# Causal attention: masking on GpSimd two units at a time, both maxima in one VectorE operation

## The reference

```
q, k, v = x @ Wq, x @ Wk, x @ Wv          # 8 batches, 16 heads of 16
dist = clip(abs(r[None, :] - r[:, None]), 0, 16)
scores = (q @ k.T) * rel_emb[dist]
scores = where(key > query, -inf, scores)
attn = softmax(scores / sqrt(16))
return (attn @ v) @ Wo + bo               # added to x, after a layernorm of x
```

## Time and profile before

| | us |
|---|---|
| median of 3 runs (3155.25 to 3163.49) | 3161.79 |
| the profiled execution's own time | 3150.57 |
| its span | 3148.8 |
| causal attention in it, first unit's scores to last | 2295.6 to 2816.7 |

### The profile page before, as it was taken

How to read it: one execution, slowest core, us unless ns; L and a number is a source line. 1 busy time by engine, 2 the same in 40 slices (tenths; PEclk the granted TensorE clock), 3 DMA queues, 4 the chain that set the end, 5 groups by cost and what they waited for, 6 DMA issues and landing times. The chain is left out here.

```text
span 3148.8 us, 54094 instructions
## 1 busy us (share of the span) xinstructions
PE 2839.0 (90%) x19481; PEld 2042.4 (65%) x19481; DVE 1666.4 (53%) x4549; ACT 1539.0 (49%) x2605; POOL 1306.5 (41%) x1303
## 2 busy tenths in 40 slices
PE   4899999758889988678999997999879999989999
PEld 3799999733344443358999996666546666655666
DVE  4411111178888888463111111666676666655666
ACT  1133333239999998311333332333257777772333
POOL 3544444349998889254444442000044444320000
PEclk9899999979999999868999998999989999998999
DMA  8199999711655555752999996000152344201000
GB/s 284 41 306 327 329 327 325 234 30 18 64 63 62 62 63 62 96 198 86 328 327 326 327 326 203 1 0 0 32 124 72 87 96 101 72 1 38 13 13 20
DMA packets 359857, 431.97 MB, mean 137 GB/s; under 512 B 86193, under 2 KB 314566, under 8 KB 356550
## 3 DMA queue, kind: packets, MB, share of 16 engines
q1 hardware_dynamic: 335046, 395.30, 45.5%
q0 software_dynamic: 24576, 33.57, 5.0%
HBM read 355.93 MB, written 72.88 MB: 136 GB/s over the span
## 5 line engine op out<-in xcount | busy, mean ns | idle before, releaser
L1675 ACT ACTIVATE f_h_t<-f_h_ps,f_b_t 128x128 f32<-128x128 f32 x1024 | 320.2, 364 | 596.3 <-PE f_h_ps L1633 596.3
L2062 POOL TENSOR_TENSOR a_dmg_buf<-a_c 128x2048 f32<-128x2048 f32 x128 | 520.1, 4091 | 85.2 <-DVE a_c L2544 42.7
L1633 PEld LDWEIGHTS f_h_ps<-f_rows_t,f_w 128*128 128x128 f32 x4096 | 481.4, 193 | 9.9 <-issue 3.5
L1633 PE MATMUL f_h_ps<-f_rows_t,f_w 128*128 128x128 f32 x4096 | 482.6, 276 | 2.3 <-DVE f_rows_t L1687 1.2
L1647 PE MATMUL f_y_ps<-f_w,f_h_t 128*128 128x256 f32 x2048 | 483.4, 379 | 0.0
L1593 POOL DMA_INDIRECT acc_rows<-f_y,f_give x128 | 205.1, 1603 | 487.2 <-DMA acc_rows<-f_y,f_give 451.6
L1647 PEld LDWEIGHTS f_y_ps<-f_w,f_h_t 128*128 128x128 f32 x2048 | 369.8, 190 | 39.9
L1687 DVE COPY f_rows_t<-f_t_ps 128x256 f32<-128x256 f32 x128 | 54.4, 425 | 598.4 <-PE f_t_ps L1621 593.7
L2411 DVE SCALAR_TENSOR_TENSOR a_bond_buf<-a_a,a_small_rep,a_q_ps 128x512 f32<-128x512 f32 x512 | 346.8, 740 | 5.3 <-PE a_q_ps L2238 2.2
L428 DVE SCALAR_TENSOR_TENSOR x_resid<-f_y_ps,f_gate,x_resid 128x256 f32 x512 | 218.8, 479 | 161.1 <-PE f_y_ps L311 155.5
L885 ACT ACTIVATE a_prob<-a_prob,a_neg_top 128x384 f32<-128x384 f32 (+3 forms) x512 | 276.5, 569 | 47.9 <-POOL a_neg_top L702 47.7
(11 more groups left out here) (337 smaller groups left out, 4110.4 us busy)
## 6 DMA issues: line engine op xcount, KB each, us to landing
f_w<-in_L_ffn_w_dram SPq DMA_DIRECT2D x256, 1024.0 KB
a_skewed<-skew SPq DMA_DIRECT2D x32, 512.0 KB, 7.2
a_k_s<-parts SPq DMA_DIRECT2D x16, 768.0 KB, 7.9
acc_rows<-x_resid SPq DMA_DIRECT2D x17, 512.0 KB, 5.3
xn_rows<-f_xn SPq DMA_DIRECT2D x16, 512.0 KB, 3.0
x_resid<-acc_rows SPq DMA_DIRECT2D x16, 512.0 KB, 8.3
a_vals<-val_rows SPq DMA_DIRECT2D x64, 128.0 KB, 4.2
skew<-a_bond SPq DMA_DIRECT2D x128, 64.0 KB
```

The lines of the kernel that those rows point to most:

```text
L1633: last = nc.tensor.matmul(h_ps[n // HB][:, (n % HB) * P:(n % HB + 1) * P], w1_sb[s][:, c, n * P:(n + 1) * P], rows_t[e % 2][:, c, :], star ...
L1675: nc.scalar.activation(h_t[k][:, n, :], h_ps[n // HB][:, (n % HB) * P:(n % HB + 1) * P], ACT.Gelu, bias=b1_t[:, n, e:e + 1]).then_inc(gelu ...
L2062: nc.gpsimd.tensor_tensor(dmg_buf[n % RING][:, :, :], places(c_sb[h], first_place(dg)), c_sb[h][:, PAD:].unsqueeze(1).broadcast_to([P, DG, ...
```

## The change

TensorE's mask product goes, and with it the masks in bfloat16. VectorE's `multiply` writes unmasked scores in two instructions: the keys left of the diagonal block with their maximum as before (not for t=0, which has none), and the diagonal block by a plain product. The maximum of the left part is put into the slot of `prob` itself, in the column just behind the block (a slot is now 513 columns wide). GpSimd then masks the diagonal blocks of an even and the following odd unit with one selection (`mask`), in place. VectorE's new `find_top` takes the maxima of both units in one reduction over the block and the column behind it, and negates them; GpSimd's `negate` is gone. ScalarE waits for the pair's maxima. The distances grow: scores s+9, multiply s+7, mask s+6, find_top s+4 (at odd s), exponential s+2 as before; `prob` has ten slots. The normalised x goes from GpSimd to ScalarE (an Identity activation with scale and bias, for which VectorE computes -mean*rstd), 28 tiles in all.

```diff
-    SCORES_AT, TTR_AT, NEG_AT, EXP_AT = 7, 5, 4, 2
-    PR = 9
+    SCORES_AT, TTR_AT, MASK_AT, TOP_AT, EXP_AT = 9, 7, 6, 4, 2
+    PR = 10
-        prob = sb("prob", [P, PR, S])
+        prob = sb("prob", [P, PR, S + 1])
 # GpSimd
-            def negate(u):
+            def mask(u):
+                t = unit(u)[1]
+                blocks = prob[:, u % PR - 1:u % PR + 1, t * P:(t + 1) * P]
                 pool.wait_ge(s_taken, UNIT_USE[u] + 1)
-                if u >= PR:
-                    pool.wait_ge(exp_ready, u - PR + 1)
-                nc.gpsimd.tensor_scalar(neg_top[:, u % PR:u % PR + 1], top[:, u % PR:u % PR + 1], -1.0, None,
-                                        ALU.mult).then_inc(top_negated, 1)
+                nc.gpsimd.affine_select(out=blocks, in_=blocks, compare_op=ALU.is_ge, fill=MASKED, base=0,
+                                        pattern=[[0, 2], [-1, P]], channel_multiplier=1).then_inc(masked, 1)
 # TensorE
                 nc.tensor.matmul(bank[:, 0:width], q_s[half % QK][0:ROWS, h, t * P:(t + 1) * P],
-                                 k_s[half % QK][0:ROWS, h, 0:width], start=True, stop=False)
-                nc.tensor.matmul(bank[:, t * P:width], ident_b[:, :], mask_b[:, :], start=False,
-                                 stop=True).then_inc(s_ready, 1)
+                                 k_s[half % QK][0:ROWS, h, 0:width], start=True, stop=True).then_inc(s_ready, 1)
 # ScalarE
-                act.wait_ge(top_negated, u + 1)
+                act.wait_ge(top_negated, u // 2 + 1)
+            def normalise(i, j):
...
+                nc.scalar.activation(xn[:, j, :], core.tile(i + 1, j), ACT.Identity, bias=less_mean[:, n:n + 1],
+                                     scale=rstd[:, n:n + 1]).then_inc(xn_ready, 1)
 # VectorE
                 if u >= PR:
                     dve.wait_ge(turned, u - PR + 1)
-                    dve.wait_ge(top_negated, u - PR + 1)
-                nc.vector.tensor_tensor_reduce(
-                    out=prob[:, u % PR, 0:width], in0=s_ps[use % SB][:, 0:width], in1=factor[:, S - width:S],
-                    scale=1.0, scalar=-3.0e38, op0=ALU.mult, op1=ALU.max,
-                    accum_out=top[:, u % PR:u % PR + 1]).then_inc(s_taken, 1)
+                if t:
+                    nc.vector.tensor_tensor_reduce(
+                        out=prob[:, u % PR, 0:t * P], in0=s_ps[use % SB][:, 0:t * P], in1=factor[:, S - width:S - P],
+                        scale=1.0, scalar=-3.0e38, op0=ALU.mult, op1=ALU.max,
+                        accum_out=prob[:, u % PR, width:width + 1])
+                nc.vector.tensor_tensor(prob[:, u % PR, t * P:width], s_ps[use % SB][:, t * P:width], factor[:, S - P:S],
+                                        ALU.mult).then_inc(s_taken, 1)
+
+            def find_top(u):
...
+                dve.wait_ge(masked, u // 2 + 1)
+                if u >= PR:
+                    dve.wait_ge(exp_ready, u - PR + 1)
+                nc.vector.tensor_reduce(neg_top[:, slots], prob[:, slots, t * P:(t + 1) * P + min(t, 1)],
+                                        AX.X, ALU.max, negate=True).then_inc(top_negated, 1)
```

More of the change, by code:

```diff
@@ L572, in attn1_phase @@
         rstd = sb("rstd", [P, TILES])
+        less_mean = sb("less_mean", [P, TILES])
         xn_t = sb("xn_t", [P, DC, S])
@@ L581, in attn1_phase @@
         v_sb = [sb(f"v{k}", [P, TPB, NH, HD + 1]) for k in range(2)]
-        prob = sb("prob", [P, PR, S])
-        wqk_sb = [prob[:, k, :].rearrange("p (c n) -> p c n", c=DC) for k in range(2)]
+        prob = sb("prob", [P, PR, S + 1])
+        wqk_sb = [prob[:, k, 0:S].rearrange("p (c n) -> p c n", c=DC) for k in range(2)]
         dist = prob[:, 2, 0:NEAR]
         hit = [prob[:, 3 + k, 0:NEAR] for k in range(2)]
-        mask_f = prob[:, 5, 0:P]
-        top = sb("top", [P, PR])
         neg_top = sb("neg_top", [P, PR])
@@ L622, in attn1_phase @@
         s_taken = sem("s_taken")
+        masked = sem("masked")
         top_negated = sem("top_negated")
@@ L672, in _ @@
         def _(pool):
[L673 to L679, removed]
             def add_bias(i, j):
@@ L717, in _ @@
                     split_low(kind, c, 0)
-            for j in range(TPB):
-                normalise(1, j)
             pool.wait_ge(rest_loaded, 32)
             for s in range(-TTR_AT, ALL):
-                if s + NEG_AT < ALL and s + NEG_AT >= 0:
-                    negate(s + NEG_AT)
+                if 0 <= s + MASK_AT < ALL and (s + MASK_AT) % 2:
+                    mask(s + MASK_AT)
                 i, m = divmod(s, UNITS)
-                if i < 0:
-                    continue
-                if m < TPB:
+                if i >= 0 and m < TPB:
                     add_bias(i, m)
-                if NORMALISE_AT <= m < NORMALISE_AT + TPB and i + 2 < B:
-                    normalise(i + 2, m - NORMALISE_AT)
                 p = product(s + TTR_AT - 1)
@@ L909, in _ @@
             root(1, TPB, LATER)
+            for j in range(TPB):
+                normalise(1, j)
             for s in range(-EXP_AT, ALL + 1):
@@ L917, in _ @@
                     root(2, LATER, TILES)
+                i, m = divmod(s, UNITS)
+                if i >= 0 and NORMALISE_AT <= m < NORMALISE_AT + TPB and i + 2 < B:
+                    normalise(i + 2, m - NORMALISE_AT)
         @block.vector
@@ L939, in inverse_std @@
                 dve.wait_ge(std_ready, count)
-                nc.vector.reciprocal(rstd[:, a:b], std[:, a:b]).then_inc(rstd_ready, 1)
+                nc.vector.reciprocal(rstd[:, a:b], std[:, a:b])
+                nc.vector.drain()
+                nc.vector.scalar_tensor_tensor(out=less_mean[:, a:b], in0=mean_var[:, a:b, 0], scalar=-1.0, in1=rstd[:, a:b],
+                                               op0=ALU.mult, op1=ALU.mult).then_inc(rstd_ready, 1)
             def take(kind, n, i):
@@ L996, in multiply @@
                     dve.wait_ge(turned, u - PR + 1)
-                    dve.wait_ge(top_negated, u - PR + 1)
-                nc.vector.tensor_tensor_reduce(
-                    out=prob[:, u % PR, 0:width], in0=s_ps[use % SB][:, 0:width], in1=factor[:, S - width:S],
-                    scale=1.0, scalar=-3.0e38, op0=ALU.mult, op1=ALU.max,
-                    accum_out=top[:, u % PR:u % PR + 1]).then_inc(s_taken, 1)
+                if t:
[6 more added lines that the diff above has]
+            def find_top(u):
+                t = unit(u)[1]
+                slots = slice(u % PR - 1, u % PR + 1)
+                dve.wait_ge(masked, u // 2 + 1)
[3 more added lines that the diff above has]
+                                        AX.X, ALU.max, negate=True).then_inc(top_negated, 1)
             def copy_o(group):
@@ L1071, in _ @@
                     multiply(s + TTR_AT)
+                if 0 <= s + TOP_AT < ALL and (s + TOP_AT) % 2:
+                    find_top(s + TOP_AT)
                 group, r = divmod(s - GU - COPY_O, GU)
```

13 lines of the change are left out of this document (4 added, 9 removed).

## The result

The changed kernel takes 3210.78 us (median of 4 runs, 3205.06 to 3219.41) where the kernel before, timed beside it, takes 3162.64 (3155.25 to 3169.56). The ratio is 1.0149 [1.0129, 1.0169]: 48 us slower. The forecast was 3186, which is 24 us slower: the direction and the place were right, and the size was half of what was measured.

What follows compares the result with a forecast made beforehand. It took a ring of hand-overs per group as the bound, TensorE being loaded less than its 98% busy. +2.6 us x 8 batches = +21, and +3 at the start, made +24: 3186 us, range 3126 to 3232.

Steps and rivals of the forecast that it cites:

- The ring: Per group of 16 units: VectorE's reduction, exponential, copy, TensorE's turn, next product, VectorE's take; 17.7 us with q and k.
- Rival 4: Slots of 513 columns start on an odd word every second time and stream more slowly: +21, 3207 us; chance 0.04.
- Why the gain does not come through: Step summing the ring of attention groups: 2 x 17.7 + 16.2 + 14.8 = 66.4 us a batch, against 64.8.
- 1 us of allowance: Added to each batch's 66.4 us for waits that a ring without reserve picks up, making 67.4.
- TensorE's part: In the ring, turns, scores, values' first part and two half products until the next k product stands: 4.7 us.
- VectorE's part: In the ring, VectorE without a pause from the k take to the last t=3 pair's reduction: 11.4 us.
- The hand-over: In the ring between VectorE's reduction and TensorE's turn: hand-over, exponential 0.63, copy 0.46 and hand-over, 1.4 us.
- At the start it forecast +3: At the phase's start, the first maximum needs five multiplied units and one reduction where it needed one: about +3 us once.
- Rivals 1 and 2: 1: banks smooth it, TensorE's saving wins, -31, 3131 us, chance 0.30. 2: both cancel, within 9 us, 3162, chance 0.12.
- rival 2: VectorE's added work falls in its waits, TensorE's saving in waits for copies: within 9 us, 3162; chance 0.12.
- Rival 3: GpSimd's mask comes late and VectorE waits for it at find_top: +42 on top of +24, 3228 us; chance 0.12.

Runs made afterwards that it cites:

- e5: The changed kernel with find_top at the head of VectorE's step and ScalarE's copy before its exponential: ratio 1.0006 to the kernel before, 3171.59 us.
- e2: The kernel before with one more VectorE product of 144 columns per unit, result unused: ratio 1.0057 to the kernel before, 3188.34 us.
- e14: The kernel before with an added 144-column VectorE product per unit and ScalarE's copy before its exponential: ratio 1.0069 to the kernel before, 3188.19 us.
- e6: The kernel before with ScalarE's copy put before its exponential, nothing else: ratio 1.0000 to the kernel before, 3168.1 us.
- e3: The changed kernel with ScalarE's copy put before its exponential in each step: ratio 1.0026 to the kernel before, 3177.4 us.
- e1: The kernel before without TensorE's mask product, scores above the diagonal left unmasked: ratio 0.9966 to the kernel before, 3162.06 us.
- e7: The changed kernel without GpSimd's selection, its signal kept, scores above the diagonal unmasked: ratio 1.0156 to the kernel before, 3216.99 us.
- e4: The changed kernel with find_top at the head of VectorE's step, ahead of take and multiply: ratio 1.0076 to the kernel before, 3191.58 us.
- e13: The changed kernel with ScalarE's copy first, find_top heading VectorE's step and one unit earlier (s+5): ratio 1.0028 to the kernel before, 3179.36 us.
- e11: The kernel before with unmasked maximum, GpSimd masking and negating pairs, scores s+8, multiply s+6, ten slots, ScalarE's copy first: ratio 0.9931, 3148.44 us.
- e9: The kernel before without mask product, maximum over unmasked rows, GpSimd masking and negating pairs, old distances: ratio 1.0019 to the kernel before, 3174.67 us.

## What of the prediction held, and the step that failed

The runs make a path from before to after in three steps. Without the mask product: 0.9966, -11 us. From there the rest of the change (VectorE's split product and reduction, the pairs, the longer distances), with both orders loose (e5, 1.0006): +13. From there both orders as in the change (1.0149): +45. The sum is +47, which is the ratio's; by the medians it is 48. The terms do not simply add: with the mask product kept and the old distances, a like load costs 18 to 22 us (e2, e14).

**The mechanism was right.** The ring was named as it stands in the trace, and the runs show it by the two edits that loosen it: 39 and 23 us, together 45, with nothing in the control e6. The exponential waits for `find_top` as forecast.

**The durations were right.** Reduction and selection came within 0.01 us. Exponentials in slots of 513 columns take 722, 613 and 509 ns for 512, 384 and 256 columns, where the kernel before has 728, 608 and 522 (the last in the earlier trace rows). Rival 4 is out. The Trainium skill (Vector Engine (DVE) Microarchitecture Reference, "Measured stream behaviour on trn2"), which it was weighed with, speaks of pairs with hops, and a contiguous run that starts on an odd word shows no such loss here.

**What failed is the step "Why the gain does not come through", its sum of the ring.** It had 66.4 us a batch and 1 us of allowance; the batch takes 71.6. TensorE's part was sized too small (the output projections left out, full clock taken for granted), VectorE's was taken as one without a pause in every group, and the ring was closed only once a group. Term by term:
- In the k group VectorE's part, from the take at 2536.62 to the end of the last reduction's share at 2547.75 (2547.41 and 0.34), is 11.13 us; forecast 11.4. The hand-over to the turn at 2549.19 is 1.44; forecast 1.4. TensorE's part until the next k take at 2554.88 is 5.69; forecast 4.7 + 0.2. The two output projections (2549.82 to 2550.28 and 2552.95 to 2553.39, 0.9 us) stand in the stretch and were not in the sum. Together 18.26 against 17.7.
- The first group of a batch, the one with the bias additions, takes 20.0 against 17.7. VectorE's part, from the take of xn at 2516.56 to 2528.55 (2528.21 and 0.34), is 11.99, where the prediction's terms make 10.6 for one take of xn and one of q. It has a pause of 0.89 in it, for the q product. The hand-over to the turn at 2530.00 is 1.45. TensorE's part until the k take at 2536.62 is 6.62, although no projection stands in it. The k group's is 4.79 without its two; the 1.8 us more fall in the stretch at a clock of 0.50. Together 20.06.
- With v products 16.97 against 16.2. Here the copies hold TensorE up by 0.23 and 0.31 us only, and the group stays at 16.88 with e3's swap and at 16.55 in e5. Most of its growth is not the ring through ScalarE, and what sets its length is open.
- With xn 16.34 against 14.8. TensorE stands three times for a copy, the first time already among the t=2 units (below). By the copies of `a_o` this group took 15.36 before the change and 15.06 without the mask product (e1). The ring sum of 14.8 is below both, so something else bounds it.

VectorE's pause in the first group, and TensorE's three in the xn group:

```profile
2526.11 0.69 DVE L950 CAST a_parts_q<-a_s_ps 128x512 bf16<-128x512 f32 x1 [0.89 <-PE a_s_ps L738]
...
2578.94 0.52 PE L770 MATMUL a_t_ps<-ident,a_prob 128*128 128x128 f32 x3 [0.84 <-ACT a_prob_t L876]
...
2584.18 0.63 PE L770 MATMUL a_t_ps<-ident,a_prob 128*128 128x128 f32 x4 [0.91 <-ACT a_prob_t L876]
...
2585.28 0.63 PE L770 MATMUL a_t_ps<-ident,a_prob 128*128 128x128 f32 x4 [0.31 <-ACT a_prob_t L876]
```

The four differences make 0.6 + 2.3 + 0.8 + 1.5 = 5.2; less the allowance of 1 that is +4.2 a batch, and 67.4 + 4.2 = 71.6. Against the kernel before the error is smaller by 0.9, since the prediction took its batch as 64.8 from the count of mask products in 400 us, and the copies say 65.7. By the copies, 400 us hold 390 units and not 395; the stretch is no whole number of batches. A sum by groups should have been set against groups.

**Smaller points.** At the start it forecast +3 and the trace has +7.3. There too the clock differs. From the first scores to the first copy it is 0.89 before the change and 0.75 now, so not all of this is the extra units:

```profile
2295.60:2330.44 34.84, 29.11 (x177) 16.26 (x176) 31.12 (x114) 22.35 (x44) 13.51 (x38) 0.89 0.50 120
2301.03:2343.42 42.39, 32.34 (x146) 16.52 (x144) 37.32 (x147) 20.41 (x41) 15.22 (x27) 0.75 0.40 99
```

VectorE was forecast busy 90% and is 78%: per unit it is busy 0.87 us and not 0.91, and the unit takes longer. TensorE's 88% was forecast as about 85%. Rivals 1 and 2 needed banks that smooth the hand-overs; e5 shows that they exist only when the order is loose, and then the result is rival 2's. Rival 3 has neither a wait in the trace nor an effect in e7.

**How much is clock.** One group of e4 prices it. Its k group has a stop of 0.90 us in each of six batches. In one of them the clock is at 0.50 for 3.4 us behind the stop, and that group takes 19.08 us where the other five take 17.52. The two windows are that group in two batches:

```profile
2538.05:2555.57 17.52, 15.67 (x108) 8.73 (x107) 14.64 (x58) 12.58 (x28) 6.63 (x13) 1.00 0.65 159
2605.88:2624.96 19.08, 17.23 (x108) 9.77 (x107) 14.72 (x58) 12.68 (x28) 6.63 (x13) 0.91 0.59 146
```

So one such stretch cost 1.56 us. The changed kernel has seven of them from 2364 to its last copy, the kernel before and e5 have none there: by this price some 11 of the +45 us are clock, an estimate. That leaves 34 for the waits themselves.

**Open.** What decides whether the clock falls behind a stop is not shown; its length alone does not (e13 has a stop of 1.42 us in each of six batches and a clock of 1.00 behind it). The last batch, without products, grew by 8 us over its five groups. Two of them, which grew by 2.97 and 2.58, hold the last two stretches at 0.50; what made up the rest is not told apart. Whether longer distances alone, with both orders as in the change, would have loosened the ring was not run.

## What to carry to other kernels

When work of two units is merged into one operation, the first unit waits for the second, and everything that is queued behind its consumer on an in-order engine waits too. Before making the merge, follow each wait back through the queues to see whether it closes on itself; if it does, put the consumer of older work ahead of the consumer of the merged result (copy before exponential: 39 us here), and lengthen the distances by what the pair adds (e11 against e9, where the copy comes first as well: 28 us). In summing such a ring, count everything that stands in each engine's queue between the two hand-overs, small projections too, and look for further places where it closes.

And before moving a mask to another engine, ask whether the maximum needs it at all: with the maximum taken over the unmasked row, the second pass on VectorE was not needed, and e11 beat both kernels, though some 10 of its 22 us are the longer distance.

## What the runs showed of the hardware

- Behind a stop of 1.43 us (busy 0.07 of 1.50 us) TensorE's granted clock was 0.50 for 3.4 us, in every steady batch of the changed kernel. Stops of 1.10 and 0.91 us in the other groups of these batches were followed by 1.00. The length of the stop does not tell it alone: in e13 the clock stayed at 1.00 behind 1.42 us (below), and in e4 it fell behind 0.90 us in one batch of six. A gap in TensorE's work may so cost more than its own length, in e4 1.56 us more.
- A matmul's mean duration says little of what it is worth. 512 mask products with a mean of 219 ns, 0.06 us from start to start, gave 11 us when removed, 0.02 each.
- A selection over two blocks costs less than two selections: GpSimd took 0.408 us for 128 x 256 and 0.293 for 128 x 128. A pair so saves 0.18 us of GpSimd, an engine that had time to spare, which is little to pay a ring for.

The stop of 1.42 us in e13's timeline, and the window from its end on, with a clock of 1.00:

```profile
2544.44 0.34 PE L759 MATMUL a_s_ps<-a_k_s,a_q_s 96*128 96x384 bf16 x1 [1.42 <-DVE x_resid L952]
...
2544.40:2550.00 5.60, 5.56 (x35) 3.68 (x36) 4.49 (x20) 3.56 (x9) 2.91 (x6) 1.00 0.99 232
```
